# VectorE reads V from the projection's PSUM bank and makes both of its halves there

## What is computed

```python
k = apply_rope(x @ Wk.T)                 # one key head, HS = 128
v = x @ Wv.T
q = apply_rope(einsum('btd,hkd->bhtk', x, Wq))      # two query heads
w = softmax(where(causal, q @ k.T * HS**-0.5, -inf))
out = (w @ v).transpose(...).reshape(B, T, 256) @ Wo.T
```

## Time and profile before

| | us |
|---|---|
| three executions | 930.96, 936.25, 939.31 |
| median | 936.25 |
| span of the profiled execution, first to last instruction | 926.4 |
| median less that span | 9.85 |

### The profile page before, as it was taken

How to read it: one execution, slowest core, us unless ns; L and a number is a source line. 1 busy time by engine, 2 the same in 40 slices (tenths; PEclk the granted TensorE clock), 3 DMA queues, 4 the chain that set the end, 5 groups by cost and what they waited for, 6 DMA issues and landing times. The chain is left out here.

```text
span 926.4 us, 15342 instructions
## 1 busy us (share of the span) xinstructions
PE 814.3 (88%) x4368; PEld 644.3 (70%) x4368; DVE 720.2 (78%) x1567; ACT 464.4 (50%) x1020; POOL 363.7 (39%) x377
## 2 busy tenths in 40 slices
PE   4689999998999989999999789988879889999952
PEld 3578788887888868888888557666656666666731
DVE  6779898896998978989978736777777878776575
ACT  2355565554565645565555255444444445444421
POOL 4535644364256434642460014333333334333331
PEclk9889999999999999999999899877897989877865
DMA  6000011101110110011000250000000100000011
GB/s 186 1 1 29 19 46 47 46 1 50 46 36 12 47 49 24 24 47 46 2 0 2 81 192 1 23 24 23 19 28 0 41 27 24 24 24 23 11 35 45
DMA packets 34588, 32.60 MB, mean 35 GB/s; under 512 B 3524, under 2 KB 34244, under 8 KB 34500
## 3 DMA queue, kind: packets, MB, share of 16 engines
q1 hardware_dynamic: 34500, 31.56, 10.7%
HBM read 16.88 MB, written 14.68 MB: 34 GB/s over the span
## 5 line engine op out<-in xcount | busy, mean ns | idle before, releaser
L507 ACT ACTIVATE pT_hi<-bank 128x512 fp32r<-128x512 f32 x192 | 90.9, 492 | 104.6 <-PE bank L843 96.1
L554 ACT ACTIVATE x_all<-scores_ps,neg_max 128x384 f32<-128x384 f32 (+7 forms) x128 | 94.6, 739 | 46.3 <-DVE neg_max L684 42.4
L580 DVE TENSOR_TENSOR pT_lo<-bank,pT_hi 128x512 fp32r<-128x512 f32 x192 | 100.7, 547 | 21.3 <-ACT pT_hi L507 21.3
L684 DVE TENSOR_REDUCE neg_max<-scores_ps 128x1 f32<-128x384 f32 (+7 forms) x128 | 95.3, 749 | 23.9 <-PE scores_ps L816 17.9
L843 PE MATMUL bank<-ident,x_all 128*128 128x128 f32 x576 | 92.7, 279 | 22.3 <-DVE pT_lo L580 17.3
L384 POOL TENSOR_TENSOR rope_a<-x_all,cos_sb 128x384 f32<-128x384 f32 x60 | 61.7, 1028 | 116.7 <-ACT x_all L507 112.6
L1342 PE MATMUL cycle_ps<-h,w_sb 128*128 128x512 f32 x192 | 92.3, 617 | 12.0 <-ACT h L1108 12.0
L843 PEld LDWEIGHTS bank<-ident,x_all 128*128 128x128 f32 x576 | 66.6, 142 | 35.4 <-DVE pT_lo L580 22.3
L1057 POOL TENSOR_TENSOR h_w<-h,w_sb 128x256 f32<-128x256 f32 x48 | 35.6, 742 | 113.1 <-ACT h L1122 113.1
L731 PE MATMUL oT_ps<-pT_hi,v_hi 128*128 128x512 f32 x192 | 77.3, 402 | 0.5 <-DVE oT_lo L580 0.4
L731 PE MATMUL scores_ps<-k_hi,q_hi 128*128 128x512 f32 (+1 forms) x192 | 71.6, 373 | 0.0
(11 more groups left out here) (132 smaller groups left out, 2120.3 us busy)
## 6 DMA issues: line engine op xcount, KB each, us to landing
x_all<-x SPq DMA_DIRECT2D x16, 512.0 KB, 3.6
out<-x_all SPq DMA_DIRECT2D x16, 512.0 KB, 3.0
x<-x_all SPq DMA_DIRECT2D x12, 512.0 KB, 3.0
x_all<-x SPq DMA_DIRECT2D x6, 1024.0 KB, 5.9
x_all<-wqkv SPq DMA_DIRECT2D x1, 512.0 KB, 4.6
sin_sb<-sin_t SPq DMA_DIRECT2D x1, 512.0 KB, 7.0
cos_sb<-cos_t SPq DMA_DIRECT2D x1, 256.0 KB, 5.8
x_all<-wo SPq DMA_DIRECT2D x1, 256.0 KB, 5.9
```

The costliest lines, as they stand in the source:

```text
L507: return nc.scalar.activation(out, in_, ACT.Copy)
L554: nc.scalar.activation(probs[u % 2][:, k, 0:keys], scores_ps[k % 2][:, 0:keys], ACT.Exp, bias=neg_max[:, u * G + k:u * G + k + 1], accum_o ...
L580: return dve.tensor_tensor(out, whole, hi.bitcast(F32), ALU.subtract)
L684: dve.tensor_reduce(neg_max[:, u * G + k:u * G + k + 1], scores_ps[k % 2][:, 0:keys], AX_X, ALU.max, negate=True).then_inc(max_ready, 1)
```

## The change

GpSimd no longer makes `v_lo`. VectorE makes `v_hi` and `v_lo` one after the other, both from the projection's PSUM bank. ScalarE copies only the 384 columns of Q and K. VectorE still waits for that copy before it reads the bank. The bank is free for TensorE when `v_lo` is made (`v_ready`), and no longer when ScalarE has copied it (`qkv_ready`).

```diff
-        qkv = [room(1) for t in range(G)]
+        qkv = [room(1)[:, 0:3 * HS] for t in range(G)]
...
-        def split_v(engine, n, i, t):
-            engine.tensor_tensor(v_lo[n][:, i, :], qkv[t][:, 3 * HS:4 * HS],
-                                 v_hi[n][:, i, :].bitcast(F32), ALU.subtract).then_inc(v_ready, 1)
+        def split_v(dve, n, i, ps, tile):
+
+            dve.tensor_copy(v_hi[n][:, i, :], ps[:, 3 * HS:]).then_inc(v_hi_ready, 1)
+            dve.wait_ge(v_hi_ready, tile + 1)
+            dve.tensor_tensor(v_lo[n][:, i, :], ps[:, 3 * HS:],
+                              v_hi[n][:, i, :].bitcast(F32), ALU.subtract).then_inc(v_ready, 1)
...
-                        if not first:
-
-                            pool.wait_ge(v_hi_ready, tile + 1)
-                            split_v(pool, n, i, t)
...
-                        at_least(act, v_ready, tile - G + 1)
-                        copy(qkv[t][:], ps[:]).then_inc(qkv_ready, 1)
+                        copy(qkv[t][:], ps[:, 0:3 * HS]).then_inc(qkv_ready, 1)
...
-                        dve.tensor_copy(v_hi[n][:, i, :], qkv[t][:, 3 * HS:]).then_inc(v_hi_ready, 1)
+                        split_v(dve, n, i, ps, bb * TILES + i)
...
-                            dve.wait_ge(v_hi_ready, i + 1)
-                            split_v(dve, n, i, t)
...
                 if kind == "project":
-                    return qkv_ready, bb * TILES + G * rest[0] + rest[1] + 1
+                    return v_ready, bb * TILES + G * rest[0] + rest[1] + 1
```

## The result

The changed kernel takes 987.9 us (median of 4, 987.03 to 988.3) against 933.61 us of the kernel before in the same session (4 runs, 928.76 to 939.31): ratio 1.0586 [1.0515, 1.0657]. It is 54.3 us slower. The forecast was 977 us in a range of 960 to 990. Executions of one kernel differ with the mean granted clock (the kernel before had a span of 931.1 us at 0.919 and one of 938.7 us at 0.902), and each ratio is given with its 95% interval and can differ by up to 0.6% from the quotient of the two medians.

A forecast was written before the change was run, and what follows sets the result against it. TensorE was taken to set the attention phase's pace. Stalls of 4 x 7.2 + 3 x 4.0 = 40.8 us on 926.4 gave a 967.2 us span, plus 9.85 to the median: 977 us, range 960 to 990.

The forecast's parts named there:

- the walk's sum: TensorE's stalls at the projections' banks, 7.2 us or 4.0 us a batch, 40.8 us in all; chance 0.50.
- what the relief is worth: GpSimd loses 28.3 us of subtractions and ScalarE 6.4 us of copying; neither is on the path, costed at nothing.
- The price of the split: VectorE's cast and subtraction from PSUM, 282 ns each; bank free 0.65 us after VectorE comes to the step.
- The rival of a longer split: `v_lo` meets GpSimd in SBUF, up to 1.1 us in place of 0.28: 982 to 992 us, chance 0.10.
- The bank's release: Attention projections: bank free only when VectorE reaches and makes both halves, so TensorE stalls; 40.8 us in all.
- project (0, 2): Next user of project (0, 0)'s bank, which comes free at 128.78 against 127.15: TensorE stalls 1.6 us.
- Turn_p (2, 2): Third transpose group, next user of project (0, 3)'s bank: at about 133.3, it stalls until 137.2.
- Turn_p (3, 2): Waits for project (1, 0)'s bank, whose cast stands behind the next x's statistics: 3.0 us stall in the 60 us batch.
- the rival of half of the stalls absorbed: VectorE catches up while TensorE stalls, so much of project (1, 0)'s stall vanishes: 966 or 960 us, chance 0.18.
- Output (1, 0): Waits for project (1, 3)'s bank, free at 170.1 against 169.40: 0.7 us stall.
- The 0.7 at turn_p (3, 3): Waits for project (1, 1)'s bank, free at 160.2 against 159.5: 0.7 us stall in the 60 us batch.
- The clock falls as well: TensorE's clock halves after the new attention-phase stalls, losing 7 to 12 us: 984 to 989 us, chance 0.16.

The follow-up runs named there:

- GpSimd's relief alone: Kernel before, with GpSimd's `v_lo` cut to 4 of its 128 columns after the first four tiles: 928.79 us, ratio 0.9962.
- the one-word experiment: The hold alone, on the kernel before: TensorE waits for VectorE's cast (`v_hi_ready`) in place of `qkv_ready` before reusing a projection's bank; 967.31 us, ratio 1.0355.
- load alone: Kernel before plus a useless VectorE maximum over 128 columns behind each cast, for which nothing waits: 944.05 us, ratio 1.0069.
- the reordered kernel: Changed kernel with a second order of VectorE's list: projects (1, 0) and (1, 1) ahead of the next x's statistics, second scale halved; 967.08 us, ratio 1.0332.

## Why the prediction was right, point by point

*What came in, and what was left out.* The mechanism and the walk's sum were right. The central 977 us is 10.9 us under the result, since it costs the clock at nothing, and the result lies inside the range because the range's upper end was drawn from two rivals, one of which came.

*What bounds, and what the relief is worth.* Right. Idle time given to TensorE became time almost one for one (+38.0 of it in the phase), and GpSimd's relief alone ends the phase at 522.1 against 522.2 us.

*The price of the split.* Right: 280 + 291 ns against 282 + 282, without spread; 0.66 us from VectorE's arrival to TensorE's start against 0.65 (its terms add up to 0.64). The rival of a longer split is out.

*The bank's release.* Right as mechanism, shown by the one-word experiment, and right in its sum: 38.1 us of idle time against 40.8. The batch of 60 us has 6.7 us more idle time (69.80 - 61.46 against 60.00 - 58.37) where 7.2 was forecast, the one of 65 us has 4.4 more where 4.0 was. Place by place in the first: project (0, 2) stalled 1.4 us where it had flowed, and ran 1.65 late (1.6 forecast). Turn_p (2, 2) added 3.05 where the walk has 2.3, as the chain from the reduction to the cast took 5.21 us (142.69 to 147.90) and not the 4.44 of before: the scale in it took 3.94 us in place of 3.18 here, and 898 ns in place of 816 in the mean over the kernel. Why it slowed is open; in the hold experiment, at 789 ns, it didn't. Turn_p (3, 2) stalled 2.66 and added 2.8 us (3.0 forecast): the statistics of x still wait for their load, 1.85 us at 169.92, and the rival of half of the stalls absorbed is out. Output (1, 0) added 0.70 (0.7). The 0.7 at turn_p (3, 3) didn't come as a stall: its bank was free at 176.18, and TensorE, at half clock behind turn_p (3, 2), came only at 176.65. So two misses of 0.7 us, one up and one down, cancel, and that the sum fits so well is in part luck.

The signs that the forecast named came a little larger: 51.7 us of waits in 32 places, the longest 3.6 us, for "some 40 us in about 30 places, the longest about 3 us"; batches of 69.8 and 71.3 us for 67 and 69. That the batches are longer than forecast is the clock: TensorE is busy 3.1 and 1.9 us longer in them. VectorE's load was called covered at +4 us, and that was too easy: it grew by 10.3 us, most of it the scale's 5.3 and `pT_lo`'s 2.8, and 6.2 us of load alone ended the phase 3.8 us later.

*The rival that should have been a term.* The forecast's 977 leaves out the clock, which "The clock falls as well" had at 984 to 989 with a chance of 0.16. Both the waits and the clock came: 38.0 us of idle time and 18.5 us of slower matmuls in the attention phase of the profiled executions. The rival too was sized too small, at 7 to 12 us. What argued against it was "most other gaps of the phase left the clock at 1.00", and this step failed. In the 60 us batch of the earlier trace rows the gaps were at most 0.94 us, so they said nothing of stalls of 2.3 and 3.0 us. Only the 65 us batches had gaps as long, and they spoke both ways: a gap of 2.21 us cost 1.7 us, while one of 2.51 us, with another of 1.95 us shortly ahead of it, left the clock at 1.00. These are its row and the stretch behind it, from the kernel before:

```profile
344.75 0.65 PE L843 MATMUL bank<-ident,x_all 128*128 128x128 f32 x4 [2.51 <-ACT x_all L507]
```

```profile
345.00:350.00 5.00, 5.00 (x33) 3.99 (x32) 3.26 (x6) 2.32 (x5) 4.62 (x6) 1.00 0.01 3
```

From such rows the fall was a chance at each of the new stalls and not a certainty, but a term of the sum all the same. Where it came, it cost about what the row of before has: scores (3, 1), from 148.97 to 151.11, took 2.14 us, and 1.37 in the kernel before, and the batch's two falls together cost the 3.1 us. In other batches it lasted longer (from 101.5 to 106.5 and from 217.5 to 222.5 us the granted clock is 0.50), where the rival counted 1.7 us a place.

*From span to median.* The 9.85 us taken as lying around the span was mostly how executions differ. (Between the medians the forecast is 40.8 us and the result 54.3.) The changed kernel's profiled execution has 987.64 us for a span of 985.8, so 1.8 us lie around it; by that the kernel before was profiled in an execution of 928.2 us, 5.4 under its median. That is why the spans differ by 59.4 us and the medians by 54.3.

*What stays open.* How the median's loss divides between wait and clock in an execution other than the profiled one; why the clock stayed full behind three of the eleven long stalls; why the scale slowed; and the low clock in the feed-forward phase of the reordered kernel.

## What to carry to other kernels

Before you let an engine read a PSUM bank in place of an earlier copy of it, walk the reader's list at each use of the bank: what counts is when that engine comes to the read, not how long the read takes. Where the walk puts stalls of 2 to 3 us on a TensorE that ran without gaps, put the clock's fall behind them into the sum and not beside it: here it came with eight of eleven long stalls and made 18.5 of the phase's 56.5 us. And relieve the engine that the bound one waits for: here the work had to leave VectorE, not to come to it.

## What the runs showed of the hardware

- A 128x128 subtraction on VectorE takes 290 to 293 ns when one input is in PSUM, whatever GpSimd does; with both inputs in SBUF 291 to 1132 ns, median 1002, beside GpSimd's rotations.
- TensorE's granted clock was 0.73 from 150 to 155 us, behind a stall of 2.88 us, and 0.84 from 175 to 180 us, behind one of 2.66 us; behind stalls of 2.86 us (at 78.72) and 2.72 us (at 314.11 and 453.91) in the same execution it was 1.00. In the kernel before, a gap of 2.21 us was followed by 0.83 over 10 us and one of 2.51 us by 1.00. The length of the stall alone doesn't tell.
- Keeping TensorE busy through the stall before turn_p (2, 2) left it at 1.00 behind that place, where it had been 0.73; at project (0, 2), where the stall was now 2.90 us in place of 1.40, it was 0.66 where it had been 1.00.
- A third VectorE instruction of 291 ns between the cast and `v_lo`, which nothing waits for, lengthened the hold of the bank by 0.19 us.
